# Value and output matrices multiplied inside the layers' first three steps instead of in a stage of their own

## The reference

```python
qkv = x @ Wqkv                       # 128 -> 3 * 1024
q, k, v = heads(qkv)                 # 16 heads of 64
q, k = rotate(l2norm(q) * qs), rotate(l2norm(k) * ksc)
attn = softmax(8 * q @ k.T)          # windows of 32, each with the window before it
out = concat(attn @ v) @ Wo          # 1024 -> 128
```

## Time and profile before

| | |
|---|---|
| median of 3 runs | 2023.24 us |
| lowest, highest | 2016.04, 2023.82 us |
| the profiled execution, its own time | 2016.79 us |
| its span (first to last instruction) | 2015.0 us |
| mean granted clock of TensorE | 0.96 |
| attention | 0 to 373 us |
| fold_values | 373 to 408 us |
| local_layers | from 408 us |

### The profile page before, as it was taken

The page is one execution under the profiler, slowest core; times in us unless marked ns, Lnnn a source line. Parts: engine busy times, 40 slices in busy tenths (PEclk is TensorE's granted clock), DMA queues, the critical chain, the costliest instruction groups (busy, mean ns, idle before and its releaser), DMA issues. The chain is left out here.

```text
span 2015.0 us, 59596 instructions
## 1 busy us (share of the span) xinstructions
PE 1808.6 (90%) x24192; PEld 1005.6 (50%) x24192; DVE 1536.6 (76%) x2543; ACT 1374.7 (68%) x2862; POOL 1262.5 (63%) x1127
## 2 busy tenths in 40 slices
PE   5898898668999999999999999999999999999974
PEld 2443444534555555555555555555555555555541
DVE  4778886247887888888888888888888888887833
ACT  1454455337887777887778877788877887778832
POOL 4303200058887777878778787787877878777710
PEclk8899999768999999999999999999999999999986
DMA  9000000224433334333333333333333333323300
GB/s 191 5 2 1 2 2 2 63 48 87 97 87 74 74 74 87 81 81 72 75 86 84 79 72 77 83 89 74 72 77 83 84 79 69 70 64 78 82 1 22
DMA packets 137216, 132.63 MB, mean 66 GB/s; under 512 B 79336, under 2 KB 82984, under 8 KB 136616
## 3 DMA queue, kind: packets, MB, share of 16 engines
q1 hardware_dynamic: 136944, 128.81, 28.8%
HBM read 20.94 MB, written 1.05 MB: 11 GB/s over the span
## 5 line engine op out<-in xcount | busy, mean ns | idle before, releaser
L1013 ACT ACTIVATE prob<-s_in,lower,rq 128x64 f32<-128x64 f32 x1536 | 543.0, 431 | 37.1 <-POOL lower L1170 36.8
L866 PE MATMUL bank_a<-x_shift,wqk_sb 128*128 128x512 f32 x768 | 375.5, 612 | 13.2 <-DVE pq L1206 8.3
L885 PE MATMUL bank_y<-zT,wvo 128*128 128x512 f32 x768 | 373.2, 609 | 1.7 <-ACT zT L1009 1.7
L1141 POOL TENSOR_TENSOR prob<-prob,rden 128x1024 f32<-128x1024 f32 x96 | 182.8, 1904 | 140.0 <-DVE rden L1216 140.0
L866 PEld LDWEIGHTS bank_a<-x_shift,wqk_sb 128*128 128x128 f32 x768 | 148.2, 196 | 198.2 <-issue 190.3
L1160 POOL TENSOR_TENSOR kfin<-rk,kfin 128x512 f32<-128x512 f32 x96 | 122.2, 1273 | 150.4 <-ACT rk L1103 101.7
L885 PEld LDWEIGHTS bank_y<-zT,wvo 128*128 128x128 f32 x768 | 137.9, 190 | 153.3 <-issue 129.9
L1009 ACT ACTIVATE zT<-bank_z 128x1024 f32<-128x1024 f32 x192 | 191.9, 1012 | 22.6 <-PE bank_z L877 22.6
L383 ACT ACTIVATE a_prob<-a_sT 128x1024 f32<-128x1024 f32 x128 | 130.5, 1023 | 104.3 <-PE a_sT L217 102.4
L492 DVE TENSOR_REDUCE a_negmax<-a_max 128x1 f32<-128x512 f32 x256 | 164.6, 684 | 46.8 <-PE a_max L167 43.0
L877 PE MATMUL bank_z<-pT,xk_prev 32*128 32x128 f32 x3072 | 166.3, 286 | 9.7 <-DVE xn L1236 5.2
(11 more groups left out here) (169 smaller groups left out, 4004.2 us busy)
## 6 DMA issues: line engine op xcount, KB each, us to landing
kpad<-kfin SPq DMA_DIRECT2D x384, 128.0 KB, 2.4
qpair<-qfin SPq DMA_DIRECT2D x384, 128.0 KB, 2.4
wqk_sb<-in_wqkv SPq DMA_DIRECT2D x40, 128.0 KB, 2.6
xk_prev<-xk_own SPq DMA_DIRECT2D x24, 192.0 KB, 2.5
ffn_sb<-in_ffn SPq DMA_DIRECT2D x6, 537.5 KB, 4.4
wv_in<-in_wqkv SPq DMA_DIRECT2D x12, 256.0 KB, 4.9
wo_in<-in_wo SPq DMA_DIRECT2D x6, 512.0 KB, 6.1
xk_prev<-xk_own SPq DMA_DIRECT2D x24, 48.0 KB, 2.7
```

What stands on the lines that cost most here:

```text
L866: last = pe.matmul(bank_a[:, half, :], wqk_sb[:, layer_of(u) % 2, part, half, g * P:(g + 1) * P], cols(u), start=True, stop=True)
L885: last = pe.matmul(bank_y[:].rearrange("p (t w q) -> p t w q", w=WPT, q=WIN), wvo[:, layer_of(u), GH * g + 2 * (hh % 2) + hh // 2, :], zT[ ...
L1013: last = act.activation(prob[:, n % 2, i, :], s_in[:, n % 2, i, :], ACT.Exp, bias=lower[:, n % 2, i:i + 1], scale=rq[:, n % 2, i:i + 1])
L1141: pool.tensor_tensor(prob[:, e % 2], prob[:, e % 2], rden[:].unsqueeze(2).broadcast_to([P, TPB * GH, 2 * WIN]), ALU.mult).then_inc(pn_ok, 1)
```

## The change

The block fold_values and its staging tensors are gone. The raw matrices are loaded into the place where the products will stand: wvo becomes six slots of 16 x 128 columns, the value matrix in columns 0 to 1023 of a slot, the output matrix in the others. Slots 0 to 2 (wvo_low) are loaded with the first weights, in the attention; slots 3 to 5 (wvo_high) by SP at the start of local_layers. The work of a layer is cut into two pieces, twelve in all; piece i is layer i // 2, pairs of heads 4 (i % 2) to 4 (i % 2) + 3. A piece is: 4 transposes into bank_y (turn_values), ACT's copy to wvT, which now lies in zT (values_turned), 8 matmuls into banks 2 and 3 of bank_z (fold), ACT's copy of the even heads and DVE's of the odd heads into the slot (even_heads, odd_heads). Steps 0, 1 and 2 of the layers do four pieces each: two groups of transposes and one product after the k projection, the rest after the q projection. The wait for POOL's constants moves behind the first product on PE and behind the second copy on ACT; POOL waits for them too.

```diff
+FOLD_STEPS = 3
-def fold_values(nc, wqkv, wo, wv_in, wo_in, loaded, wvo, ident):
...
+def value_parts(slot, wqkv, wo, layer):
+    raw = slot.rearrange("p h c -> p (h c)")
+    to = raw[:, 0:INNER].rearrange("p (q a d) -> p a q d", a=2, d=DH)
+    parts = []
+    for a in range(2):
+        at = 2 * INNER + a * (INNER // 2)
+        parts += [(to[:, a], wqkv[layer][:, at:at + INNER // 2].rearrange("p (q d) -> p q d", d=DH))]
+    return parts + [(raw[:, INNER:2 * INNER], wo[layer])]
...
+        wvT = zT[:].rearrange("p a w t h q -> p (a w t h q)")[:, 0:2 * INNER].rearrange("p (l q c) -> p l q c", l=2, c=P)
...
 SP:
+            for layer in range(STAGED, DEPTH):
+                for part in value_parts(wvo[layer], wqkv, wo, layer):
+                    sp.dma_start(*part).then_inc(vo_loaded[layer], 16)
             sp.wait_ge(prev_zero, 1)
...
 PE:
+            def turn_values(i):
+                layer, q = divmod(i, 2)
+                after(pe, vo_loaded[layer], 0, 48)
+                after(pe, wvT_ok, i - 1)
+                for k in range(PAIRS // 2):
+                    last = pe.matmul(bank_y[:, k * P:(k + 1) * P], raw_values(layer, 4 * q + k), ident[:],
+                                     start=True, stop=True, is_transpose=True)
+                last.then_inc(vturn_mm, 1)
+
+            def fold(i):
+                layer, q = divmod(i, 2)
+                after(pe, wvT_ok, 2 * layer + 1)
+                after(pe, even_ok, i - 1)
+                after(pe, odd_ok, i - 1)
+                for k in range(PAIRS // 2):
+                    for a in range(2):
+                        rows = slice(64 * a, 64 * a + 64)
+                        last = pe.matmul(bank_z[:, 2 + a, k * P:(k + 1) * P], wvT[rows, layer % 2, 4 * q + k, :],
+                                         raw_outputs(layer, 4 * q + k)[rows], start=True, stop=True)
+                last.then_inc(fold_mm, 1)
...
                     project(n, 1, k_mm)
+                if s < FOLD_STEPS:
+                    turn_values(4 * s)
+                    turn_values(4 * s + 1)
+                    if s == 2:
+                        after(pe, xk_ok, 0)
+                    fold(4 * s)
+                if s == 0:
+                    pe.wait_ge(const_ok, 1)
...
                     project(n, 0, q_mm)
+                if s < FOLD_STEPS:
+                    fold(4 * s + 1)
+                    turn_values(4 * s + 2)
+                    turn_values(4 * s + 3)
+                    fold(4 * s + 2)
+                    fold(4 * s + 3)
+                if s == FOLD_STEPS:
+                    after(pe, even_ok, 4 * FOLD_STEPS - 1)
+                    after(pe, odd_ok, 4 * FOLD_STEPS - 1)
...
                 if u_rows is not None:
+                    if s < FOLD_STEPS:
+                        after(pe, even_ok, 4 * s + 3)
                     turn(bank_z[:, 2, :], lambda t: tile_cols(u_rows, t), xk_mm)
...
-            pe.wait_ge(const_ok, 1)
...
 ACT:
+            def values_turned(i):
+                after(act, vturn_mm, i)
+                after(act, fold_mm, 2 * (i // 2 - 1) - 1)
+                at = slice(4 * (i % 2), 4 * (i % 2) + 4)
+                copy(wvT[:, i // 2 % 2, at].rearrange("p q c -> p (q c)"), bank_y[:]).then_inc(wvT_ok, 1)
+
+            def even_heads(i):
+                after(act, fold_mm, i)
+                copy(half_heads(i, 0), bank_z[:, 2, :].rearrange("p (k c) -> p k c", c=P)).then_inc(even_ok, 1)
...
                         act.activation(sq[:, 0, :], bank_a[:, 0, :], ACT.Square).then_inc(sqk0_ok, 1)
+                    if s < FOLD_STEPS:
+                        values_turned(4 * s)
                     if quarter(d):
                         exponentials(d, 2, 6)
                     if quarter(n):
                         after(act, pk2_ok, n)
                         act.activation(sq[:, 1, :], bank_a[:, 1, :], ACT.Square).then_inc(sqk_ok, 1)
+                    if s < FOLD_STEPS:
+                        values_turned(4 * s + 1)
+                    if s == 0:
+                        act.wait_ge(const_ok, 1)
...
                         act.activation(rk[:], rk[:], ACT.Exp, scale=-0.5).then_inc(rk_ok, 1)
+                        if s < FOLD_STEPS:
+                            even_heads(4 * s)
...
+                if s < FOLD_STEPS:
+                    even_heads(4 * s + 1)
+                    values_turned(4 * s + 2)
+                    values_turned(4 * s + 3)
+                    even_heads(4 * s + 2)
+                    even_heads(4 * s + 3)
...
 POOL:
             last.then_inc(const_ok, 1)
+            pool.wait_ge(const_ok, 1)
...
 DVE:
+            def odd_heads(i):
+                after(dve, fold_mm, i)
+                dve.tensor_copy(half_heads(i, 1), bank_z[:, 3, :].rearrange("p (k c) -> p k c", c=P)).then_inc(odd_ok, 1)
...
                     first_products(n, 1, pk).then_inc(pk_ok, 1)
+                if s < FOLD_STEPS:
+                    odd_heads(4 * s)
...
                     dve.tensor_reduce(s_max[:], s_in[:, c % 2], AX.X, ALU.max, negate=True).then_inc(max_ok, 1)
+                if s < FOLD_STEPS:
+                    for i in range(4 * s + 1, 4 * s + 4):
+                        odd_heads(i)
```

More of the change, by code:

```diff
@@ L709, in local_layers @@
 def local_layers(nc, args, state, held):
-    wqkv, ffn = args
+    wqkv, ffn, wo = args
     x_shift, ident, halfneg, eps = state
-    (wqk_sb, wvo, ffn_sb, scale_sb, rot_sb, mask_sb), (qk_loaded, ffn_loaded, const_in) = held
+    (wqk_sb, wvo, ffn_sb, scale_sb, rot_sb, mask_sb), (qk_loaded, ffn_loaded, const_in, vo_loaded) = held
     with ExitStack() as ctx:
@@ L775, in local_layers @@
             sem, ["sumk_ok", "sumq_ok", "rotk_ok", "kfin_ok", "qfin_ok", "pn_ok", "eps_ok", "rstd_ok"])
+        vturn_mm, wvT_ok, fold_mm, even_ok, odd_ok = map(sem, ["vturn_mm", "wvT_ok", "fold_mm", "even_ok", "odd_ok"])
         kpad_in, qpair_in, prev_in = sem("kpad_in"), sem("qpair_in"), sem("prev_in")
@@ L816, in tile_cols, with raw_values, raw_outputs, half_heads @@
             return x_shift[:, at:at + P]
+        wvT = zT[:].rearrange("p a w t h q -> p (a w t h q)")[:, 0:2 * INNER].rearrange("p (l q c) -> p l q c", l=2, c=P)
+        def raw_values(layer, p):
+            return wvo[layer].rearrange("p h c -> p (h c)")[:, p * P:(p + 1) * P]
+        def raw_outputs(layer, p):
+            return raw_values(layer, PAIRS + p)
+        def half_heads(i, a):
+            at = 8 * (i % 2) + a
+            return wvo[i // 2][:, at:at + 7:2, :]
         block = ctx.enter_context(nc.Block())
@@ L1467, in attention_then_local_layers @@
         ffn_sb = sb("ffn_sb", [P, 2, FFN_COLS])
-        staging = ctx.enter_context(ExitStack())
-        wv_in = staging.enter_context(nc.sbuf_tensor("wv_in", [P, STAGED, INNER], F32, side="right"))
-        wo_in = staging.enter_context(nc.sbuf_tensor("wo_in", [P, STAGED, PAIRS * P], F32, side="right"))
+        wvo_low = sb("wvo_low", [P, STAGED, HEADS, P])
         qk_loaded, ffn_loaded = (ctx.enter_context(nc.semaphore(n)) for n in ("qk_loaded", "ffn_loaded"))
-        vo_loaded = [ctx.enter_context(nc.semaphore(f"vo{k}_loaded")) for k in range(STAGED)]
+        vo_loaded = [ctx.enter_context(nc.semaphore(f"vo{k}_loaded")) for k in range(DEPTH)]
         first_weights = []
         for k in range(STAGED):
-            first_weights += [(*value_half(wv_in, k, A["wqkv"], k, a), vo_loaded[k]) for a in range(2)]
-            first_weights += [(wo_in[:, k], A["wo"][k], vo_loaded[k])]
+            first_weights += [(*part, vo_loaded[k]) for part in value_parts(wvo_low[:, k], A["wqkv"], A["wo"], k)]
         for part in range(2):
@@ L1495, in attention_then_local_layers @@
                         first_weights)
-        wvo = sb("wvo", [P, DEPTH, HEADS, P])
-        fold_values(nc, A["wqkv"], A["wo"], wv_in, wo_in, vo_loaded, wvo, ident)
-        staging.close()
-        local_layers(nc, (A["wqkv"], A["ffn"]),
+        wvo_high = sb("wvo_high", [P, DEPTH - STAGED, HEADS, P])
+        wvo = [wvo_low[:, k] for k in range(STAGED)] + [wvo_high[:, k] for k in range(DEPTH - STAGED)]
+        local_layers(nc, (A["wqkv"], A["ffn"], A["wo"]),
                      (x_shift, ident, halfneg, eps), ((wqk_sb, wvo, ffn_sb, scale_sb, rot_sb, mask_sb),
-                                                      (qk_loaded, ffn_loaded, const_in)))
+                                                      (qk_loaded, ffn_loaded, const_in, vo_loaded)))
         last_norm(nc, out, x_shift, x1_tok, ident, halfneg, eps)
```

61 lines of the change are left out of this document (1 added, 60 removed).

## The result

The changed kernel takes 1999.0 us in the median of 6 runs (1994.5 to 2007.0), the kernel before 2017.3 us in 6 runs beside it (2015.4 to 2023.8). The ratio is 0.9903 (95% interval 0.9879 to 0.9927), 14.7 to 24.4 us less; measured again in the experiments it was 0.9925 (0.9903 to 0.9947). Its profiled execution took 1996.8 us. The forecast was 14 us less, 2009.2 us, within 1996 to 2021.

The account below looks back on a forecast made before the run. TensorE, 90% busy, bounds the kernel, with the stage a serial stretch. Removing 36.9 us and lengthening three steps from 46.6 to 70.3 gains 13.2, with step 3 14: 2009.2 us from the 2023.2 median, range 1996 to 2021.

Parts of the forecast that it names:

- Removed, 36.9 us: Before the layers: the serial stage's 34.9 us and PE's 2.0 us wait for the constants go.
- Added, by the walk: Steps 0 to 2, followed operation by operation with the pieces: 58.3 us all high, 84.3 all low, 46.6 before.
- low walk: Step 0 followed at the low clock, 1.2 GHz: 24.0 us, PE 84% busy, q projection until 14.2.
- longest added wait: Step 2's first fold, waiting for ScalarE's copy of the own rows; said to hold only what is in the sum.
- The clock: Granted clock in steps 0 to 2 taken as the removed stage's 0.77: steps 70.3 us, gain 13.2 us.
- Step 3: The fourth step gets some 0.8 us back, as a wait for the late q sum goes; total gain 14 us.
- The signs of being wrong: A wait over 3 us before a fold, a load ending one, or another step length from the fifth on.
- Costed at nothing: Nine loads at the block's start, issue under 10 us, cover nothing; VectorE's twelve copies lie in its waits.
- Low or high throughout: Clock rivals for steps 0 to 2: low, gain about 0, 2023 (0.22); high, gain 26, 1997 (0.10).
- Slower: Rival: clock stays low past the fourth step, some 10 to 12 us more per step; chance 0.05.
- late weights: Rival: loads at a third of the rate hold step 1's folds some 5 us, 2014; chance 0.03.
- low case: Rival: clock stays low for the first three steps, gain about 0, 2023; chance 0.22.

Follow-up runs that it names:

- own_early: Changed kernel with ScalarE copying step 2's own rows and second transposed group before four exponentials and a square; one execution, 2003.1 us.
- fill_wait: Changed kernel with two extra unused matmuls of 512 columns on PE during step 2's wait for the copy of the own rows; one execution, 2002.1 us.
- after_again: The changed kernel unedited, measured once more; ratio to the kernel before 0.9925 (0.9903 to 0.9947).
- loads_late: Changed kernel with SP issuing the nine loads of layers 3 to 5 behind step 0's k and q transfers; one execution, 2001.3 us.
- spare_banks: Changed kernel with second-half transposes and product in other free banks, both transposed groups copied before the even heads; ratio to the kernel before 0.9849.
- all_three: Changed kernel with spare banks, early own rows, and step 2's last four exponentials behind three copies; 1982.5 us, 0.9833 of the kernel before.
- const_first: Changed kernel with PE waiting for GpSimd's constants before its first projection again; one execution, 2013.9 us.
- best: Changed kernel with spare banks, early own rows, later exponentials, two banks for first-half transposes and an earlier second copy; 1984.4 us, 0.9835 of the kernel before.
- plain_turns: Changed kernel with the 48 added transposes as plain matmuls against the identity; one execution 1989.7 us, timed again at ratio 0.9867 to the kernel before.

## Why the prediction was right, point by point

**Removed, 36.9 us.** Right: the first projection starts at 373.04, 0.04 us after the block, where it stood at 409.93. The 37.9 us of the run without pieces agree, but hold some 4 us of shorter steps and some 3 of a longer stretch behind them.

**Added, by the walk.** The order of the waits was right, one by one, and their sizes at the high clock too (7.7 us for 7.5 in the second half of step 0). At the clock of 0.77 the walk gave 70.3 us for the three steps; they took 68.7 at 0.80. Its step starts give near 20, 24 and 26 us. Step 0 took 21.4 (its first half ran low: the q projection ended 13.7 us after the start, 14.2 in the low walk); step 1 took 20.2, at 1.00 throughout, where the walk's high value is 20.0; step 2 took 27.1 (its fold, pick, scores and head sums at the low clock). So the one mean was spread evenly over steps that ran at either level, and the misses of 1.6, -4.2 and 1.0 us cancel to -1.6 in the sum. The sentence that step 2's fold has the longest added wait was wrong: it is 2.04 us, and 2.75 stand before the last transposes.

**The clock.** Its mean came out at 0.80 for 0.77. That it lies between the levels was argued from the low walk's busy share (84%; over the three steps PE was busy for 75%, 51.3 of 68.7 us); that the removed stage's own value would be so near was luck. With the same pieces in the steps the runs of this case gave 0.79 to 0.97, by where the clock rose and fell. The prediction left open whether transposes count for it and gave that no price; with plain matmuls the three steps were 3.3 us shorter.

**Step 3.** It was to give 0.8 back and gave 2.5 (12.78 us for 15.24). The wait for the late q sum, 0.73 us before, is gone, as forecast, though a wait of 1.63 for POOL's k sum stands in the step now; the rest is the clock, 0.92 over the step for 0.66. A stall of 2.1 us in step 5, with the low clock behind it, made steps 4 to 8 2.2 us longer than before, where the stall in that step was of 1.5. At step 8 the gain is 15.1 us for 14, and that it is so near is luck in part: the steps gave 1.6 more than the sum, step 3 1.7 more, and the stall took 2.2 back.

**The signs of being wrong.** None came: no wait over 3 us stands before a fold, no load ends a wait of PE in the steps, and away from the stall the later steps keep their length (13.53 us from the head sums of step 7 to those of step 8, 13.52 before).

**Costed at nothing.** Right for the loads, by the run with the loads behind step 0. The sum of their issue was wrong, though: three of 2.2 us and six of 1.1 are 13.2, not under 10, and that is later than the 9 us at which the first k transfer was due. The longest single issue took 3.1 us, the nine together 9.5 (373.00 to 382.50), and nothing came of it, since the first k transfer is issued only at 387.83:

```profile
376.29 3.10 SPq L816 DMA_DIRECT2D wvo_high<-in_wo  x1
...
380.57 1.93 SPq L816 DMA_DIRECT2D wvo_high<-in_wo  x1
```

DVE's copies are in the chain where the walk had them, in the wait of 0.89.

**The total.** By medians 18.2 us, by ratio 19.6 and in the second measurement 15.1, for 14. The 20 us between the two profiled spans are 15.1 at step 8 and 4.9 behind it. Behind step 8 the changed kernel took 1475.2 us in one execution and 1485.6 in the other, the kernel before 1480.0, so these 4.9 us are within what executions of one kernel differ by. The median came out at 1999 and not 2009 for this, and because of the kernel before: its six runs had a median of 2017.3, 6 us under the three that the forecast was put on.

**Rivals.** Low or high throughout did not happen; the clock was low for some 12 us from 373, 9 from 421 and 5 from 437. Slower and late weights did not happen. With plain matmuls in place of the transposes the clock was higher, 0.95 for 0.80, as the Trainium skill's rule ("TensorE: Matmul & The Clock Gate", Part 4: PE-mode transpose) has it. That cost 3.3 us in the steps, and not the 14 between forecast and low case.

## What to carry to other kernels

Moving a serial stage under other work pays only its own chain's length less what is stretched: here 37.9 us were removed and 22.7 put back, since the pieces shared one bank and one pair of banks and took turns with the copies. Look for banks that are idle at that moment before judging such an overlap; here they gave another 13 us at the mark. A wait of PE can cost more than its own length by the low clock behind it: in own_early two waits shorter by 2.1 us together gave 4.3. A run with the wait filled tells whether such a low stretch is saved or only moved, as in fill_wait. And read single profiles to the point where executions begin to differ: behind it two executions of one kernel were 10 us apart.

## What the hardware showed unexpectedly

**Transposes and the clock.** With 48 transposes of 128x128 replaced by plain matmuls of twice the records, the granted clock of the three steps was 0.95 for 0.80, in two executions, and the steps 3.3 us shorter. The first rise shows it best. In seven executions with transposes whose first projection started between 371.7 and 373.8 us (changed, after_again, fill_wait, own_early, loads_late, spare_banks, all_three), the clock stayed at 0.50 for over 12 us from that start; in the two with plain matmuls, started at 373.0 and 373.2, for less than 6. The Trainium skill's page named above states the rule, and these runs agree with it; the trace of before could not show it. Two things limit this. The plain matmuls also keep PE busy for longer, and no run tells that from their kind. And const_first and best, both with transposes, started at 375.1 and 374.7 and were at 1.00 within 4 us, by the time their first transposes began, and the transposes of step 0 did not bring the clock down.

**Stalls in the score matmuls.** In some steps PE stands for some 2 us in the row of 128 score records with no releaser, and the clock is often low just behind. One in the changed kernel's timeline:

```profile
473.87 1.39 PE L860 MATMUL bank_z<-kpad,qpair 64*32 64x64 f32 x116
477.34 0.33 PE L860 MATMUL bank_z<-kpad,qpair 64*32 64x64 f32 x12 [2.08 <-issue]
477.60 1.86 PE L940 MATMUL bank_f<-sumk,same_head 128*128 128x512 f32 x2
479.25 2.89 PE L827 MATMUL bank_a<-x_shift,wqk_sb 128*128 128x512 f32 x4
```

The head sums behind it take 1.86 us and the projection 2.89 instead of 1.12 and 1.88. After 450 us the kernel before has 5 such stalls of over 1.5 us in the scores, the changed one 3, and the changed kernel again 6, at a span of 2003.7 us against 1995.0 with marks that agree within 0.4 us. So two executions of one kernel end 8.7 us apart after the same first steps; the added stalls and the low clock behind them are what the two traces show for it. They are not spread at random: the scores of step 5 have one in twelve of the fourteen traces (1.2 to 2.2 us), whatever the edit, and only the two with plain matmuls have none there. From the head sums of step 4 to those of step 6 the changed kernel took 30.7 us, plain_turns 27.1, so one stall with the low clock behind it is worth up to 3.6 us, and it lies inside the mark. What causes them no run here shows.
